# Graph network kernel: node-by-edge one-hots made on VectorE in the score stage, values stored by tile

## What is computed

```python
k, q, v = (typed_linear(x, ntype, W) for W in (Wk, Wq, Wv))    # (n, 8 heads, 16)
kw = einsum('nhd,htdo->nhto', k, Watt)[src, :, etype]          # one row of a table by (node, type)
m  = einsum('nhd,htdo->nhto', v, Wmsg)[src, :, etype]          # the value half of the same row
a  = einsum('ehd,ehd->eh', kw, q[dst]) * pri[:, etype].T / sqrt(16)   # score stage
att = edge_softmax(a, dst, n)                                          # softmax stage
hag = segment_sum((m * att[:, :, None]).reshape(-1, 128), dst, n)      # message stage
```

## Time and profile before

| Engine | busy us | share of span | instructions |
|---|---|---|---|
| TensorE, products | 3237.8 | 48% | 14685 |
| TensorE, weight loads | 2275.6 | 34% | 14685 |
| VectorE | 2192.8 | 33% | 5075 |
| ScalarE | 1125.1 | 17% | 2416 |
| GpSimd | 3200.5 | 48% | 3406 |

### The profile page before, as it was taken

One profiled execution on the slowest core, in us unless ns is written; L12 is line 12 of the kernel. 1 busy time (PEld: TensorE's weight loads), 2 busy tenths in 40 slices (PEclk: granted clock), 3 DMA queues, 4 the chain that ended last, 5 costly groups with the idle time before them and its releaser, 6 DMA issues. The chain is left out here.

```text
span 6705.1 us, 60482 instructions
## 1 busy us (share of the span) xinstructions
PE 3237.8 (48%) x14685; PEld 2275.6 (34%) x14685; DVE 2192.8 (33%) x5075; ACT 1125.1 (17%) x2416; POOL 3200.5 (48%) x3406
## 2 busy tenths in 40 slices
PE   4545477757773445533353335634334255343353
PEld 3333344435542223332332222223334222233243
DVE  2113122322223223411121124423338444233385
ACT  0001122312222101100010002301004323011053
POOL 4664566456644665366546652066630410655302
PEclk7666677767786667755575557766667677666676
DMA  2111334323332332211131127944434489444343
GB/s 60 46 47 36 79 101 101 85 74 101 102 95 73 90 84 71 106 44 46 41 127 46 47 59 304 407 115 127 127 103 117 136 332 384 116 123 125 99 130 103
DMA packets 600928, 772.14 MB, mean 115 GB/s; under 512 B 89734, under 2 KB 507000, under 8 KB 588064
## 3 DMA queue, kind: packets, MB, share of 16 engines
q1 hardware_dynamic: 480000, 492.16, 21.9%
q0 software_dynamic: 120608, 276.12, 15.5%
HBM read 416.10 MB, written 351.82 MB: 115 GB/s over the span
## 5 line engine op out<-in xcount | busy, mean ns | idle before, releaser
L444 POOL DMA_INDIRECT arena<-table,idx_s x3128 | 2980.7, 953 | 2539.0 <-issue 870.8
L712 PE MATMUL ps<-arena,onehot 128*128 x4160 | 912.0, 367 | 904.3 <-issue 518.1
L712 PEld LDWEIGHTS ps<-arena,onehot 128*128 128x128 f32 x4160 | 774.7, 265 | 1146.9 <-issue 1146.3
L422 DVE TENSOR_TENSOR onehot<-ps,dl_s 128x512 f32<-128x512 f32 x416 | 278.8, 684 | 979.6 <-remote 695.8
L426 DVE TENSOR_SCALAR onehot<-iota_row,dl_s,w_s 128x128 f32<-128x128 f32 x1248 | 347.9, 356 | 459.4 <-remote 374.9
L1892 PE MATMUL ps<-ident,onehot 128*128 128x128 f32 x832 | 192.2, 375 | 612.6 <-DVE onehot L422 346.6
L1852 DVE TENSOR_TENSOR arena<-arena,ps 128x128 f32<-128x128 f32 x832 | 183.8, 282 | 827.8 <-remote 617.0
L883 DVE SCALAR_TENSOR_TENSOR arena<-ps,vecs,arena 128x256 f32<-128x256 f32 x208 | 100.6, 484 | 964.3 <-ACT arena L862 533.4
L1903 PE MATMUL ps<-arena 128*128 x1664 | 328.7, 361 | 179.4 <-issue 130.3
L1903 PEld LDWEIGHTS ps<-arena 128*128 128x128 f32 x1664 | 295.5, 267 | 212.9 <-issue 211.0
L1892 PEld LDWEIGHTS ps<-ident,onehot 128*128 128x128 f32 x832 | 134.8, 193 | 644.3 <-DVE onehot L422 362.8
(11 more groups left out here) (336 smaller groups left out, 3887.2 us busy)
## 6 DMA issues: line engine op xcount, KB each, us to landing
table<-arena SPq DMA_DIRECT2D x96, 2048.0 KB
values<-arena SPq DMA_DIRECT2D x832, 64.0 KB
arena<-values SPq DMA_DIRECT2D x208, 256.0 KB
arena<-table,idx_s POOLq DMA_INDIRECT x3128
arena<-edge_times SPq DMA_DIRECT2D x208, 128.0 KB
edge_part<-arena SPq DMA_DIRECT2D x208, 128.0 KB
table<-arena SPq DMA_DIRECT2D x50, 512.0 KB
arena<-edge_part SPq DMA_DIRECT2D x98, 256.0 KB
```

Of the source, the lines that this page charges most:

```text
L422: is_dst = dve.tensor_tensor(onehot[:, 4 * q:4 * q + 4, :], iota.unsqueeze(1).to_broadcast([P, 4, P]), dl_s[:, ds(j, 4)].unsqueeze(2).to_b ...
L444: pool.indirect_dma_start(ring[:, ds(t % RING * 2 * H, width)], None, tab, bass.IndirectOffsetOnAxis(ap=idx_s[:, t:t + 1], axis=0)).then_i ...
L712: mm = pe.matmul(accf[:, ds(b, P)], o, ring[:, ds(slot, H)], start=False, stop=False, skip_group_check=True)
```

## The change

The setup also writes the edge targets as floats to HBM (`dst_rows`) and computes `node_s` (block x 128 + partition, for each step). In the score stage SyncE loads the targets of four tiles at a time, broadcast to all 128 partitions, into a ring of 60 tiles (`dst_ring`), and VectorE compares them with `node_s`: the result is the node-by-edge one-hot itself, one instruction for each step. It works five groups ahead, in eight buffers; TensorE's products have all eight PSUM banks. Transposes and ScalarE's copies go. Values are stored by tile, four tiles in one DMA with fixed addresses, and `freed` waits for the one store of the slot. In the message stage SyncE therefore reads the tile numbers of four steps into registers and loads four tiles with one DMA each.

```diff
         edge_part = dram("edge_part", [SHARE_TILES, P, H])
-        values = dram("values", [STEPS, P, H])
+        values = dram("values", [4 * TILE_QUADS, P, H])
+        dst_rows = dram("dst_rows", [E])
...
+        node_s = sb("node_s", [P, STEPS])
...
-        XT = sb("XT", [P, NP])
-        Hn = sb("Hn", [P, NB, H])
-        HF = sb("HF", [P, NP])
+        work = sb("work", [P, 3 * NP])
+        XT, HF = work[:, 0:NP], work[:, 2 * NP:3 * NP]
+        Hn = work[:, NP:2 * NP].rearrange("p (b f) -> p b f", f=H)
...
+                sp.wait_ge(made.sem, 1)
+                sp.dma_start(dst_rows.rearrange("(p c) -> p c", p=CROWS), dst_f).then_inc(dst_out.sem, 16)
...
-                ch(dve.tensor_scalar(turn_f, turn_f, float(2 * H), None, ALU.mult))
+                ch(dve.tensor_scalar(turn_f[0:32, :], turn_f[0:32, :], float(2 * H), None, ALU.mult))
+                ch(dve.tensor_scalar(turn_f[64:96, :], turn_f[64:96, :], float(H), None, ALU.mult))
                 ch(dve.memset(slot_i[:, STEPS:STEPS + 4], 0))
                 ch(dve.tensor_copy(slot_i[:, 0:STEPS], turn_f))
+                ch(dve.tensor_copy(slot_i[32:64, 0:STEPS], slot_f[32:64, :]))
...
+                ch(dve.tensor_scalar(node_s[:, :], blk128, chunk_f[:, 0:1], None, ALU.add))
...
+        def step_tiles(eng, regs, j):
+
+            eng.load(regs, slot_i[32:33, ds(j, len(regs))])
+            return [eng.snap(r, min_val=0, max_val=EDGE_TILES - 1) for r in regs]
...
+                dst_ring = work[:, 0:RING * H]
+                Qn_flat = Qn.rearrange("p b f -> p (b f)")
+                homes = [onehot[:, 4 * r:4 * r + 4, :] for r in range(QUADS)]
+                homes += [arena[:, 6528 + 512 * r:7040 + 512 * r].rearrange("p (c e) -> p c e", c=4) for r in range(2)]
+                homes += [work[:, 7680 + 512 * r:8192 + 512 * r].rearrange("p (c e) -> p c e", c=4) for r in range(2)]
+                DEPTH, BANKED, BEFORE, SKEW = len(homes), 8, 8, 5
...
-                        stored_quads = [-1]
-
-                        def freed(pool, n):
+                        def freed(pool, n, k):
                             pool.wait_ge(mixed.sem, mixed.at(n + 1))
-                            for m in range(stored_quads[0] + 1, n + 1):
-                                pool.wait_ge(ring_out[m % QUADS].sem, ring_out[m % QUADS].at(64 * (m // QUADS + 1)))
-                            stored_quads[0] = n
+                            pool.wait_ge(ring_out[k % QUADS].sem, ring_out[k % QUADS].at(16 * (k // QUADS + 1)))
                         gathers(pool, table32, 2 * H, freed)
...
-                        def body(i, first):
-                            for q in range(QUADS):
-                                n = i * QUADS + q
-                                if not first:
-                                    sp.wait_ge(ring_out[q].sem, ring_out[q].at(64 * i))
-                                slots = step_slots(sp, sp_cols, n * 4)
-                                sp.wait_ge(arrived.sem, step_need(sp, n) + arrived.base)
-                                for c in range(4):
-                                    sp.dma_start(values[ds(n * 4 + c, 1), :, :].rearrange("a e f -> (a e) f"),
-                                                 ring[:, ds(slots[c] + H, H)]).then_inc(ring_out[q].sem, 16)
-                        trips(sp, body)
-                        for q in range(QUADS):
-                            sp.wait_ge(ring_out[q].sem, ring_out[q].at(64 * TRIPS))
+                        pairs = ring.rearrange("p (r c) -> p r c", c=2 * H)
+
+                        def load(k):
+                            if 4 * k >= RING:
+                                sp.wait_ge(onehot_ready.sem, onehot_ready.at((4 * k - RING + 3 + NB - 1) // 4 + 1))
+                            first, last = 4 * k * P, min(E, 4 * (k + 1) * P)
+                            at = 4 * k % RING * P
+                            sp.dma_start(dst_ring[:, at:at + last - first], dst_rows[first:last].partition_broadcast(P)).then_inc(row_in[k % U].sem, 16)
+
+                        def store(k):
+                            n = min(4, EDGE_TILES - 4 * k)
+                            sp.wait_ge(arrived.sem, arrived.at(k + 1))
+                            if k >= QUADS:
+                                sp.wait_ge(ring_out[k % QUADS].sem, ring_out[k % QUADS].at(16 * (k // QUADS)))
+                            sp.dma_start(values[4 * k:4 * k + n, :, :].rearrange("t e f -> e t f"),
+                                         pairs[:, 4 * k % RING:4 * k % RING + n, H:2 * H]).then_inc(ring_out[k % QUADS].sem, 16)
+                        for k in range(BEFORE):
+                            load(k)
+                        for k in range(TILE_QUADS):
+                            store(k)
+                            if k + BEFORE < TILE_QUADS:
+                                load(k + BEFORE)
...
+                        def onehots_across(n):
+                            if n < TILE_QUADS:
+                                dve.wait_ge(row_in[n % U].sem, row_in[n % U].at(16 * (n // U + 1)))
+                            if n >= DEPTH:
+                                dve.wait_ge(made.sem, made.at(n - DEPTH + 1))
+                            rows = step_rows(dve, dve_rows, n * 4)
+                            for c in range(4):
+                                is_dst = dve.tensor_scalar(homes[n % DEPTH][:, c, :], dst_ring[:, ds(rows[c], P)], node_s[:, ds(4 * n + c, 1)],
+                                                           None, ALU.is_equal)
+                            is_dst.then_inc(onehot_ready.sem, 1)
...
-                                product = dve.tensor_tensor(prod[:, q % 2, c, :], ring[:, ds(slots[c], H)], ps[:, 4 + q, c * P:(c + 1) * P], ALU.mult)
+                                product = dve.tensor_tensor(prod[:, n % 2, c, :], ring[:, ds(slots[c], H)], ps[:, n % BANKED, c * P:(c + 1) * P], ALU.mult)
...
+                        for n in range(SKEW):
+                            onehots_across(n)
+                        for n in range(ALL_QUADS):
+                            if n + SKEW < ALL_QUADS:
+                                onehots_across(n + SKEW)
+                            multiply(n)
+                            if n > 0:
+                                reduce(n - 1)
 
                     @block.tensor
                     def _(pe):
-                        def turn(i, q, fresh):
-                            n = i * QUADS + q
+                        for n in range(ALL_QUADS):
+                            blocks = step_blocks(pe, n * 4, 4)
                             pe.wait_ge(onehot_ready.sem, onehot_ready.at(n + 1))
-                            if not (fresh and q < 2):
-                                pe.wait_ge(evac.sem, evac.at(n - 1))
-                            for c in range(4):
-                                mm = pe.transpose(ps[:, q % 2, c * P:(c + 1) * P], onehot[:, 4 * q + c, :], ident[:, :])
-                            mm.then_inc(quad_done.sem, 1)
-
-                        def query(i, q, fresh):
-
-                            n = i * QUADS + q
-                            blocks = step_blocks(pe, n * 4, 4)
-                            pe.wait_ge(evac.sem, evac.at(n + 1))
-                            if not fresh:
-                                pe.wait_ge(mixed.sem, mixed.at(n - 3))
+                            if n >= BANKED:
+                                pe.wait_ge(mixed.sem, mixed.at(n - BANKED + 1))
                             for c, b in enumerate(blocks):
-                                mm = pe.matmul(ps[:, 4 + q, c * P:(c + 1) * P], onehotT[:, q % 2, c * P:(c + 1) * P],
-                                               Qn_flat[:, ds(b, P)], start=True, stop=True)
+                                mm = pe.matmul(ps[:, n % BANKED, c * P:(c + 1) * P], homes[n % DEPTH][:, c, :], Qn_flat[:, ds(b, P)], start=True, stop=True)
                             mm.then_inc(made.sem, 1)
-
-                        def body(i, first):
-                            for q in range(QUADS):
-                                turn(i, q, first)
-                                if not (first and q < 1):
-                                    query(i if q >= 1 else i - 1, (q - 1) % QUADS, first)
...
                                     sp.wait_ge(mixed.sem, mixed.at(i * QUADS + q - 3))
-                                sp.dma_start(vals[:, 4 * q:4 * q + 4, :],
-                                             values[ds(i * U + 4 * q, 4), :, :].rearrange("a e f -> e a f")).then_inc(ring_in[q].sem, 16)
+                                tiles = step_tiles(sp, sp_cols, i * U + 4 * q)
+                                for c in range(4):
+                                    sp.dma_start(vals[:, 4 * q + c, :],
+                                                 values[ds(tiles[c], 1), :, :].rearrange("a e f -> (a e) f")).then_inc(ring_in[q].sem, 16)
...
```

(2 more changed lines are left out.)

65 lines of the change are left out of this document (26 added, 39 removed).

## The result

Four runs of the changed kernel against four of the kernel before, on one chip: the median of the changed kernel is 6972.3 us, that of before 6688.1 us. The ratio is 1.0413, with a 95% interval of 1.0395 to 1.0431: the change makes the kernel 4.1% slower. One of the four took 7182.6 us at a granted clock of 0.524, the slower state that this program has in some executions; it is in the median and not in the ratio, and the median of the other three is 6967.0 us. The profiled execution took 6967.0 us (span 6965.3 us, granted clock 0.636), 260 us more than the profiled one of before.

What follows compares the result with a forecast made beforehand. Bound taken: SyncE's late value stores hold the score stage's gathers. From the profiled 6706.9 us, -127 (score stages) +266 (message stages) +1 (setup) gives 6847, or 6828 us by the median; range 6710 to 7010 us.

Steps and rivals of the forecast that it cites:

- (b): Score stage: fixed-address stores by tile take the store wait off the gather path; pass 565 us, between 551 and 583.
- (c): Score stage, VectorE: 2.5 us a group, 8 to 10 groups left after the last gather, tail 27 us.
- (d): Message stage: SyncE's register read and four loads take 2.40 us a group and become the bound; together +266 us.
- (e): Setup, once: edge targets written to HBM and three short VectorE instructions added; +1 us (0 to 2).
- (a): Score stage: transposes on TensorE and their copies on ScalarE go; counted at nothing by itself.
- rival 2: Score stage keeps its length, pauses ended by VectorE instead of the store; 6955 us by the median; 15 in 100.
- rival 3: Score stage: VectorE's SBUF-only one-hots stop GpSimd, adding 285 us to the forecast; 7112 us; 4 in 100.
- Rival 4: Message stage: SyncE's queue keeps up with the present 1.12 us, leaving only the gain; 6562 us; 7 in 100.
- Rival 1: Score stage: gathers never pause, 504 us per stage, a gain of 303 us; 6652 us by the median; 8 in 100.

Runs made afterwards that it cites:

- e12: Kernel before, only the score stage's stores changed: values stored by tile at fixed addresses, one-hots and transposes kept; pausing chip, 6621.4 us, ratio 0.9888.
- e10: Changed kernel, message stage reading sixteen tile numbers with one register read per four groups; pausing chip, 6944.6 us, ratio 1.0378.
- e8: Changed kernel, but values stored by step from ScalarE's queue, two VectorE reads merged, message stage of before; pausing chip, 6659.3 us, ratio 0.9952.
- e4: Changed kernel without VectorE's register reads in the score stage (fixed columns, constant wait); chip without pauses, 6084.5 us, ratio 1.0564.
- c0: Kernel before, unaltered, traced again on a chip without pauses, where the kernel before took 5759 to 5761 us.
- c1: Changed kernel, unaltered, run again on a chip without pauses: 6075.8 us, ratio 1.0545 against the kernel before.
- e11: The kernel of e4 once more, meant for a pausing chip but run on one without pauses: 6085.7 us, ratio 1.0566.
- e2: Kernel before, each message-stage group load of 256 KB made into four 64 KB loads at fixed addresses: 5937.5 us, ratio 1.0313.
- e1: Changed kernel, message stage loading each group with one 256 KB DMA at a fixed address: 5769.5 us, ratio 1.0018.

## Why the prediction was right, and where not

Forecast 6828 us, measured 6972 us: the sign and the balance of one gain and one larger loss are right, and the time is in the range, 38 us below its upper end. The loss itself is 284 us, twice the 140 us forecast. By its own steps, in the two profiled executions:

| Step | Forecast, us | Measured, us |
|---|---|---|
| (b) score pass | 565 | 585.3, 584.4 |
| (c) tail | 27 | 43.6, 43.6 |
| (b), (c) both layers | -127 (-177 to -61) | -58 |
| (d) message stage, both layers | +266 (+221 to +395) | +315 |
| (e) rest | +1 | +4 |

That is 69 us too much gain, 49 us too little loss and 3 us, 121 of the 144 us. The next 19 us are the step from profile to median: the profiled execution of before was 18.6 us above its median, and I took that off; the changed kernel's was not above its own. The last 5 us lie between that execution and the median of the four. The +4 us of (e) are no cost of the setup: the first gather of the program starts at 63.6 us, where it started at 63.4 us.

(a) That the transposes and copies are worth nothing by themselves holds: e12, which keeps them, has a shorter score stage than the changed kernel and than e10.

(b) The mechanism is right: the store left the gather path and SyncE no longer crawls (its stores last 0.388 us in the median; the earlier trace rows had 0.699). The size failed in one choice, 565 us between the passes at 551 and 583 us. Eight score passes on such a chip with SyncE's stores by step gone, of four different kernels (the changed one, e8, e10, e12), took 578 to 586 us. The row that I named as the upper bound, the pass whose ring VectorE frees, was the one like it.

(c) Two terms failed. The first is that three register reads "run beside" the work. They are in VectorE's own in-order stream: a group with one-hots took 3.5 to 4.0 us instead of 2.5, and e4, without the reads, 2.2. The second is the number of groups left at the last gather, 14 and not 8 to 10. Over all 14 a group took 3.1 us, so the number is worth about 10 us and the length about 8. The one-hots ahead make the length (e12, with VectorE's loop as before, has a tail 10 us shorter), and they don't make the number: 14 and 15 are left in e12 without them. Fourteen groups of four tiles are nearly the whole ring of 60: on a pausing chip VectorE is a ring behind the gathers, and it is a few groups behind on the others (c0, c1). Before the change the late stores held the gathers back, so that only 8 and 5 groups were left. That the reads alone account for the tail on a pausing chip was not run: e11 was to show it, and its chip didn't pause.

(d) Right in mechanism, a tenth short in size. A start with a register address took 0.52 us where I had 0.47, the read with its register work 0.44 us where I had 0.54, and a group 2.64 us in place of 2.40; the last 0.1 us is a start of over 1 us now and then, for which I had nothing. My bounds count 0.50 us for the read where the text has 0.54, which is 8 us, and by the sum the sign turns at a score stage of 522 us, not 519. e2 splits the cost: 88 us a layer for four DMAs instead of one, 65 us for reads and addresses. The nearest rows were those of stores, and a load is not quite one.

The rivals. The measured time is nearer to rival 2's 6955 us than to the forecast. Half of what it says came true: the pauses' releaser changed from the store to VectorE, and with it more than half of the expected gain went. But the stage didn't keep its length, and without the message stage's extra 49 us the time would lie between the two. GpSimd was not held by VectorE's one-hots (rival 3): its median gather is 0.946 us in both kernels on the first chip, and on a chip without pauses, where nothing else holds the pass, the pass went from 488.6 to 491.6 us (c0, c1), where rival 3 has 142 us a layer. The warning of the Trainium skill (SBUF — State Buffer, section SBUF: two separate sides) doesn't show for these one-hots; whether they ran in a two-port mode no run shows. Rival 4 is out by e1 and e2. Rival 1, gathers that never pause, is what c1 shows, though not through the change: there the kernel before doesn't pause either, and the gain is not 303 us but nothing. I had read the pauses as the kernel's own. Every pass had them, also those without a store by step, and that was the hint that something other than the store made them. The forecast's gain therefore held only by the chip that it was measured on: on the other sort the ratio is 1.0545, where the forecast's times give 1.021.

On the first chip an engine crawled, and the change moved the crawl to another engine. VectorE in the changed kernel, while gathers stream:

```profile
4605.60 0.29 DVE L1896 TENSOR_TENSOR arena<-arena,ps 128x128 f32<-128x128 f32 x1 [2.88 <-issue]
4606.31 0.29 DVE L1896 TENSOR_TENSOR arena<-arena,ps 128x128 f32<-128x128 f32 x1 [0.43 <-issue]
4607.01 0.29 DVE L1896 TENSOR_TENSOR arena<-arena,ps 128x128 f32<-128x128 f32 x1 [0.41 <-issue]
```

Three multiplies of 0.29 us stand 0.71 and 0.70 us apart. Before, it was SyncE's stores that stood so the earlier trace rows, and not VectorE's multiplies. In e12 neither engine does it, and the passes are still 583 and 578 us. So such a crawl is not needed for the pauses. What makes them on one sort of chip and not on the other was not found; no edit here touches it.

## What to carry to other kernels

Count a moved addressing by the queue that has to do it: one DMA made into four with addresses from registers cost 1.5 us for each group of four steps here, with the same bytes, and only a queue with that much slack can hide it. A register read is an instruction in its engine's stream: on VectorE one of four registers took 0.56 us, where four one-hots took 0.93. And before a pause is priced as a gain, look whether passes that have nothing to do with the supposed cause pause too, and time the kernel before on another chip.

## What the runs showed of the hardware that I had not expected

- The same program took 5760 us on some chips and 6690 us on others, each within 0.4%, with the gathers themselves equally long (0.946 and 0.949 us). Of the 938 us between the two traces of the kernel before, 610 lie in the eight gather passes, which pause on the one sort of chip; signals come late there, and on some engines instructions stand 0.7 us apart while the gathers stream. Where the other 328 us lie is known only for the two tails after the score passes, 64 us.
- Reads into registers: four took 0.296 us on SyncE and 0.56 us on VectorE, eight 0.816 us on VectorE, sixteen 0.971 us on SyncE; but two took 0.476 us on SyncE and 0.505 us on GpSimd. Why two took longer than four on SyncE is open.
- With an address from a register, GpSimd starts a plain 64 KB load in 0.534 us, SyncE in 0.333 us; from start to start it is 0.59 us on GpSimd and 0.52 us on SyncE.
